# A relational graph layer on one core: edge types by transfer, a third buffer of relation rows, and one-hots in another place

## What is computed

```python
def _mgcn_conv(x, edge_index, edge_type, rel, W_in, W_out, W_loop, b, n):
    src, dst = (edge_index[0], edge_index[1])
    e = edge_index.shape[1]
    half = e // 2
    m = x[src] * rel[edge_type]
    m = jnp.concatenate([m[:half] @ W_in, m[half:] @ W_out], 0)
    deg = jax.ops.segment_sum(jnp.ones((e,), x.dtype), dst, num_segments=n)
    norm = 1.0 / jnp.maximum(deg, 1.0)
    agg = jax.ops.segment_sum(m * norm[dst][:, None], dst, num_segments=n)
    return jnp.tanh(agg + x @ W_loop + b)
...
h = emb + res * _mgcn_conv(emb, edge_index, edge_type, rel1, ...)
h = h + res * _mgcn_conv(h, edge_index, edge_type, rel2, ...)
return h @ mu_w + mu_b
```

## Time and profile before

| | us |
|---|---|
| median of three runs | 2800.0 (2799.91 to 2800.91) |
| span of the one profiled execution | 3183.3 |
| of it, edges of layer 0 and of layer 1 | 1236.8 and 1228.1 |
| of it, all other stages | 718.4 |

### The profile page before, as it was taken

The page is one execution under the profiler, slowest core; times in us unless marked ns, Lnnn a source line. Parts: engine busy times, 40 slices in busy tenths (PEclk is TensorE's granted clock), DMA queues, the critical chain, the costliest instruction groups (busy, mean ns, idle before and its releaser), DMA issues. The chain is left out here.

```text
span 3183.3 us, 55393 instructions
## 1 busy us (share of the span) xinstructions
PE 2759.1 (87%) x20688; PEld 2587.3 (81%) x20688; DVE 2303.9 (72%) x3258; ACT 1865.5 (59%) x3179; POOL 1952.0 (61%) x2129
## 2 busy tenths in 40 slices
PE   4888888888888888797888888888888887997998
PEld 3888888888888888796877887878777786997998
DVE  6777777777677777896777777777777776995665
ACT  6556665555555555585555555555555554785444
POOL 6666666666666666455666666666666664892223
PEclk9999989999999999899999999999999999998999
DMA  8333333333333333353333333333333333452221
GB/s 259 119 90 89 89 89 90 89 89 90 88 89 90 90 88 90 92 164 104 90 90 90 89 90 92 88 90 90 89 89 92 88 90 98 136 158 90 69 67 64
DMA packets 162458, 312.57 MB, mean 98 GB/s; under 512 B 34061, under 2 KB 95309, under 8 KB 162229
## 3 DMA queue, kind: packets, MB, share of 16 engines
q0 software_dynamic: 79872, 218.21, 23.8%
q1 hardware_dynamic: 81120, 89.89, 8.8%
q10 hardware_dynamic: 1237, 1.41, 0.2%
HBM read 263.90 MB, written 45.48 MB: 97 GB/s over the span
## 5 line engine op out<-in xcount | busy, mean ns | idle before, releaser
L740 PE MATMUL edge_rg<-edge_rel_hi,edge_hot 128*128 128x256 f32 x6656 | 1551.7, 293 | 86.6 <-issue 63.0
L740 PE MATMUL edge_rg<-edge_rel_lo,edge_hot 128*128 128x256 f32 x4992 | 1312.3, 289 | 60.0 <-issue 58.9
L740 PEld LDWEIGHTS edge_rg<-edge_rel_hi,edge_hot 128*128 128x128 f32 x6656 | 1219.6, 197 | 143.7 <-issue 92.2
L548 ACT ACTIVATE edge_hot<-edge_typ,minus_type 128x512 fp32r<-128x512 f32 x832 | 526.8, 685 | 935.9 <-DMA dense_prev<-emb_t 383.9
L740 PEld LDWEIGHTS edge_rg<-edge_rel_lo,edge_hot 128*128 128x128 f32 x4992 | 983.1, 197 | 70.0 <-issue 68.5
L623 DVE TENSOR_TENSOR edge_m_lo<-edge_rg,edge_m_hi 128x1024 fp32r<-128x1024 f32 x416 | 509.3, 1224 | 241.3 <-ACT edge_m_hi L541 127.7
L604 DVE TENSOR_SCALAR edge_hot<-edge_typ,type_of 128x512 fp32r<-128x512 f32 x832 | 582.3, 741 | 12.4 <-ACT edge_hot L548 8.7
L753 PE MATMUL edge_small<-edge_m_hi,edge_sel 128*128 128x258 f32 x1664 | 458.1, 306 | 96.3 <-DVE edge_m_lo L623 90.7
L530 POOL DMA_INDIRECT edge_xg<-emb,src x416 | 399.0, 959 | 225.9 <-issue 96.2
L530 POOL DMA_INDIRECT work<-h,src x416 | 400.7, 963 | 221.9 <-issue 101.9
L530 POOL DMA_INDIRECT edge_xg<-h,src x416 | 400.2, 962 | 216.2 <-issue 102.8
(11 more groups left out here) (183 smaller groups left out, 3933.9 us busy)
## 6 DMA issues: line engine op xcount, KB each, us to landing
work<-emb,src POOLq DMA_INDIRECT x416
edge_xg<-emb,src POOLq DMA_INDIRECT x416
work<-h,src POOLq DMA_INDIRECT x416
edge_xg<-h,src POOLq DMA_INDIRECT x416
set_x_rows<-in_x SPq DMA_DIRECT2D x25, 256.0 KB, 3.9
emb<-set_e_rows SPq DMA_DIRECT2D x25, 256.0 KB, 2.9
emb_t<-acc SPq DMA_DIRECT2D x5, 1280.0 KB
dense_prev<-emb_t SPq DMA_DIRECT2D x25, 256.0 KB, 2.7
```

Of the source, the lines that this page charges most:

```text
L548: act.activation(hot[:, q % 2, c], typ[q % 2][:], ACT.Abs, bias=K["minus_type"][:, c:c + 1]).then_inc(distances, 1)
L740: ins = pe.matmul(rg[q % 2][:, t, :], hot[:, q % 2, c, t * P:(t + 1) * P], part[:, c, :], start=(c == 0 and part is rel_hi), stop=(c == FULL))
```

## The change

- **Types.** The set-up stores the edge types as 16-bit integers, and SP loads those of a pair (1024 numbers) into all 128 partitions, into a tile `typ` of two buffers in SBUF, one transfer of 256 KB a pair. PE's matmul for it goes, and so do two PSUM buffers. DVE's one-hots no longer wait for ACT's distances but for that transfer, and explicitly for the relation rows that read `hot` before.
- **Three buffers of relation rows** (`RG_RING`) in place of two, in the PSUM that became free. GpSimd's gather now also waits for the message that last read its place in the ring; ACT's high part also waits for the window that last read its buffer.
- **Lags.** Message, select and low part come three turns after the one-hots (two before), the window sums five (four), the transposes and the adding six (four). PE's first window of a pair also waits for the adding of the pair before the last.
- **Order in a turn.** DVE's one-hots stand between message and select, no longer behind the low part; ACT starts its turn with the copy of the sums and the high part.

```diff
+RG_RING = 3
+SUMS_LAG = 5
+TURN_LAG = 6
...
-            act.copy(K["typ"][0:TYPE_ROWS], types_i[0:TYPE_ROWS]).then_inc(tables, 1)
+            act.copy(types_s[0:TYPE_ROWS], types_i[0:TYPE_ROWS]).then_inc(types_short, 1)
+            act.wait_ge(types_short, 1)
+            act.dma_start(types_out, types_s[0:TYPE_ROWS]).then_inc(types_stored, 16)
...
+        typ = s.sb("typ", [P, 2, 2 * GROUP * P], I16)
...
-        rg = [s.ps(f"rg{b}", [P, GROUP, DIM]) for b in range(2)]
-        typ = [s.ps(f"typ{b}", [P, GROUP * P]) for b in range(2)]
+        rg = [s.ps(f"rg{b}", [P, GROUP, DIM]) for b in range(RG_RING)]
...
+            def load_types(p):
+
+                wait_past(sp, hot_done, 2 * p - 2)
+                wait_past(sp, distances, HOT_ACT * (2 * p - 2))
+                sp.dma_start(typ[:, p % 2], types[p:p + 1, :].rearrange("o k -> (o k)").partition_broadcast(P))\
+                  .then_inc(typ_in[p % 2], 16)
...
+                wait_past(pool, messages, g - GROUPS_IN_RING + 1)
                 for t in range(GROUP):
...
+                    if bank is by_three:
+                        wait_past(act, windowed, g - 1)
...
-                act.wait_ge(typ_done, g + 1)
+                act.wait_ge(typ_in[q // 2], 16 * (i + 1))
+                wait_past(act, rel_done, g - 1)
...
-                over_groups(act, (0, later(distance)), (2, high), (0, later(one_hot)), (3, copy_sums), (0, clear_one))
+                over_groups(act, (SUMS_LAG, copy_sums), (3, high(by_three)), (0, later(distance)), (0, later(one_hot)),
+                            (0, clear_one))
...
-                dve.wait_ge(distances, HOT_ACT * (g + 1))
-
+                dve.wait_ge(typ_in[q // 2], 16 * (i + 1))
+                wait_past(dve, rel_done, g - 1)
                 for c in range(HOT_ACT, RCHUNKS):
-                    ins = dve.tensor_scalar(hot[:, q % 2, c], typ[q % 2][:], K["type_of"][:, c:c + 1], None,
+                    ins = dve.tensor_scalar(hot[:, q % 2, c], types_of(q), K["type_of"][:, c:c + 1], None,
                                             ALU.is_equal)
...
-                over_groups(dve, (2, message), (2, one_window), (4, add_window), (2, low), (0, one_hot_later))
+                over_groups(dve, (3, message(by_three)), (0, one_hot_later), (3, one_window), (TURN_LAG, add_window),
+                            (3, low(by_three)))
...
-                pe.matmul(typ[q % 2][:], row, K["typ"][0:TYPE_ROWS, q % 2 * GROUP * P:(q % 2 + 1) * GROUP * P],
-                          start=True, stop=True).then_inc(typ_done, 1)
...
+                    if q % 2 == 0:
+                        wait_past(pe, added, g // 2 - 1)
...
-                over_groups(pe, (4, one_window), (2, relation_rows), (0, spread_later), (4, turn_over))
+                over_groups(pe, (SUMS_LAG, one_window), (TURN_LAG, turn_over), (2, relation_rows(by_three)))
```

More of the change, by code:

```diff
@@ L427, in over_groups, with phase_edges @@
         turn(STEPS + t // GROUPS_IN_RING, t % GROUPS_IN_RING)
-def phase_edges(nc, K, layer, nodes, rel, nodes_t, matrices):
+def phase_edges(nc, K, layer, types, nodes, rel, nodes_t, matrices):
     first = layer == 0
@@ L465, in phase_edges @@
         rel_split = s.sem("rel_split")
-        picked = s.sem("picked")
-        typ_done = s.sem("typ_done")
+        typ_in = [s.sem(f"typ_in{b}") for b in range(2)]
         gathered = [s.sem(f"gathered{q}") for q in range(GROUPS_IN_RING)]
@@ L477, in phase_edges @@
         filled = s.sem("filled")
-        summed = s.sem("summed")
+        windowed = s.sem("windowed")
         sums_copied = s.sem("sums_copied")
@@ L505, in _ @@
                                  columns(K, chunks).rearrange("p c k n -> p c (k n)")).then_inc(columns_out, 16)
+            for p in range(2, PAIRS):
+                load_types(p)
             sp.wait_ge(messages, GROUPS - 2)
@@ L560, in copy_sums @@
                 if q % 2 == 1:
-                    act.wait_ge(summed, g // 2 + 1)
+                    act.wait_ge(windowed, g + 1)
                     act.copy(sums_sb[:, q // 2], sums[q // 2][0:WIN, :]).then_inc(sums_copied, 1)
@@ L689, in all_windows @@
                         add(0, w * WIN, half_at + w * WIN).then_inc(win_added, 1)
-                over_groups(dve, (0, pick_row), (2, message), (2, low), (0, one_hot_later), (3, all_windows),
+                over_groups(dve, (2, message(by_two)), (0, one_hot_later), (2, low(by_two)), (3, all_windows),
                             rolled=True)
@@ L726, in spread_later, with relation_rows, stage @@
-            def spread_later(g, q, i):
-                if not isinstance(g, int) or g > 1:
-                    spread_types(g, q, i)
-            def relation_rows(g, q, i):
-                if isinstance(g, int) and g == 0:
-                    pe.wait_ge(rel_split, 3)
-                    pe.wait_ge(filled, 3)
-                pe.wait_ge(hot_done, g + 1)
-                pe.wait_ge(hot_act, g + 1)
-                for t in range(GROUP):
-                    for c in range(RCHUNKS):
-                        for part in (rel_hi, rel_lo) if c < FULL else (rel_hi,):
-                            ins = pe.matmul(rg[q % 2][:, t, :], hot[:, q % 2, c, t * P:(t + 1) * P], part[:, c, :],
-                                            start=(c == 0 and part is rel_hi), stop=(c == FULL))
-                    if t < GROUP - 1:
-                        ins.then_inc(rel_tile, 1)
-                ins.then_inc(rel_done, 1)
+            def relation_rows(bank):
+                def stage(g, q, i):
+                    if isinstance(g, int) and g == 0:
+                        pe.wait_ge(rel_split, 3)
+                        pe.wait_ge(filled, 3)
+                    pe.wait_ge(hot_done, g + 1)
+                    pe.wait_ge(hot_act, g + 1)
+                    rows = rg[bank(g, q)]
+                    for t in range(GROUP):
+                        for c in range(RCHUNKS):
+                            for part in (rel_hi, rel_lo) if c < FULL else (rel_hi,):
+                                ins = pe.matmul(rows[:, t, :], hot[:, q % 2, c, t * P:(t + 1) * P], part[:, c, :],
+                                                start=(c == 0 and part is rel_hi), stop=(c == FULL))
+                        if t < GROUP - 1:
+                            ins.then_inc(rel_tile, 1)
+                    ins.then_inc(rel_done, 1)
+                return stage
@@ L1579, in build @@
 def build(nc, a, out):
+    types = nc.dram_tensor("types", [TYPE_ROWS, 2 * GROUP * P], I16, kind="Internal").ap()
     emb = nc.dram_tensor("emb", [NODES_PAD, DIM], F32, kind="Internal").ap()
```

82 lines of the change are left out of this document (42 added, 40 removed).

## The result

The changed kernel takes **2886.5 us** (2885.1 to 2887.0), the kernel before 2800.5 beside it: 1.0306 times as long, 95% interval 1.0291 to 1.0320. It is slower by 86 us. I had forecast slower at 2822, that is +22 with a range of 2670 to 2900: the sign and the range held, the size did not.

A forecast was written before the change was run, and what follows sets the result against it. GpSimd's gathers were taken to bound the kernel at 5.0 us a group, before and after. 2800 + 2 (layer starts) + 20 (one more window that delays gather starts) = 2822 us, range 2670 to 2900.

The forecast's parts named there:

- The bound: Edge stages: GpSimd's gathers set the pace, 4 x 1.25 = 5.0 us a group, with PE and DVE just below.
- 2080 + 718: Whole kernel before: 1664 gathers at 1.25 us plus the stages outside the edges, 2798 us against a median of 2800.
- Types, one-hots, third buffer, lags: PE and DVE in the edges: savings hidden under GpSimd's floor, worth 0; lag at most one turn, 5 us, a layer.
- New waits and SP's queue: Edges: waits of gathers and ACT's copy worth 0; SP's 208 transfers, 55 MB, hidden.
- 2 us for the starts of the layers: Layer starts: two type transfers ahead of the relation table, 0 to 3.9 us a layer, taken as 1, 2 us in all.
- The price of the gathers: Edges: gathers starting inside a select or SBUF one-hot are lengthened; net 20 us, bounds 0 and 146.
- net one window, 20 us: DVE in the edges: three windows instead of two, each catching 0.28 starts a group at 0.175 us, over 416 groups.
- 963 against 0.95: Gathers of before: mean 963 ns against 0.95 us, 22 us over 1664, taken to agree with 20 us for one window.
- C: Rival: GpSimd's and DVE's rhythms lock, a start falls into a one-hot's window every group; 73 to 146 us; chance 0.10.
- forecast A: The forecast itself: GpSimd bounds the kernel before and after; 2785 to 2860 us; chance 0.62.
- B: Rival: PE and DVE bound the timed runs, so the change is faster, 2592 or 2654 us; chance 0.25.
- D: Rival: one-hots also stop gathers in progress, 0.53 us a group, 221 us, 3021 us; chance 0.03.

The follow-up runs named there:

- first profile: Profile of the unchanged kernel before, taken ahead of the forecast: span 3183 us against a median of 2800.
- cut kernels: Changed kernel and kernel before, each without one of four gathers a group from the fifth group on: 2568.0 us after, 2705.0 before.
- run with the free place: Changed kernel with the select ahead of the message, waiting for the third of its group's four gathers: 2815.0 us, 1.0051.
- second profile: Kernel before, unchanged, profiled once more: span 2798.1 us.
- run with two transfers a layer: Changed kernel with type transfers for only the first two pairs of each layer (206 of 208 left out): 2885.8 us, 1.0301.
- run with DVE's old order: Changed kernel with DVE's order of before: message, select, adds, low part, one-hots: 2916.2 us, 1.0414.

## Why the prediction was right in sign and wrong in size

**The bound.** Right, and now shown and not only inferred: the 383 us of the first profile belonged to that one execution, 2080 + 718 is the time of before, and the cut kernels move with the gathers.

**Types, one-hots, third buffer, lags.** Right: worth 0 together under GpSimd's floor, within the few microseconds that the run with the free place leaves. The low part's wait of the earlier trace rows fell from 223 us (second profile) to 3.5, the one-hots take 482 ns in the median (480 forecast), and PE's and DVE's gains are there. They show only where GpSimd has room: 2705 to 2568, where I had put DVE's chain at 4.77 and PE at 4.5 a group and the runs have 4.76 and 4.4.

**New waits and SP's queue.** Right at 0: idle time between gathers is unchanged, and the run with two transfers a layer has the same time. The transfers land in 3.3 us, those of the earlier trace rows in 3.9:

```profile
edge_typ<-types SPq DMA_DIRECT2D x208, 256.0 KB, 3.3
```

I had 2 us for the starts of the layers. No run shows this term: of the 2.3 us by which the profiles differ outside the edges, 2.2 lie in the last stage.

**The price of the gathers: the step that failed.** This is the term "net one window, 20 us". The delay of one start was right (a start waits until some 0.13 us before DVE's instruction ends; 0.21 us each in after). Wrong was the number of starts: I spread them evenly and let a window catch 0.28 of them, 20 us for one window more. They are not spread. With GpSimd in the lead each start has its fixed place after the message, and a window catches one in most groups or in hardly any: 12 of 416 for before's select (2 us), 357 for after's (76 us), and 45 for the one-hots (6 us). So the term measures some 80 us in place of 20; the gathers as a whole became 81 us longer. The agreement that I leaned on, with 963 against 0.95, came from the disturbed execution, where late releases had shaken the phases: 145 starts inside selects there, 12 in the second profile. It agreed for the wrong reason.

**The rivals.** C had the mechanism (rhythms lock, because a message waits for its gather) and the price: 73 to 146 us, measured 86. It named the wrong instruction. The one-hots moved into the free place at 1.1 to 2.05 us and pushed the select out of it. I gave it 0.10, although the rule "GpSimd leads and the message waits for its landing" was in my own forecast A and makes locking the normal case. B falls with the cut kernels.

D, that gathers in progress stop too, was rightly low: the gather of 804.42 ran through a one-hot's start and took 0.94, and of the 331 in after that were 0.1 to 0.3 us under way when a pair of one-hots began none took more than 0.96. The Trainium skill, SBUF — State Buffer, section Who interferes with whom, tells of a lock that falls to whoever issues first. I had left this condition out when I took D for that rule: by it a gather in progress would hold back the one-hots. The traces show little of that: the pair at 804.60, which began during a gather, took 1.01 us in place of 0.88. The section also says that an instruction with two SBUF inputs contends with a GpSimd instruction that reads SBUF, and one in a mode that uses both ports with GpSimd at large, while one with at most one SBUF input outside those modes doesn't contend. The traces agree for the select, which held starts back with both inputs in SBUF and not with one in PSUM, and for message, low part and adds, which held back none. The SBUF one-hots held starts back and the PSUM one-hots didn't; whether the former run in such a mode, no run here shows.

**Could it have been forecast?** Nearly; one number was missing. Pitch 1.25, and a message 2.75 us behind the start of its last gather, give starts at 1.0, 2.25, 3.5 and 4.75 us. Message 1.13 and two one-hots of 0.48 put the select at 2.09, with the start at 2.25 in it. The select would end at 2.57 and let the gather begin 0.13 earlier, at 2.44: 0.19 x 416 = 79 us, a time of 2879, which is near 2886. The 2.75 was not in a row of mine, since the first profile had hardly a group in step.

## What to carry to other kernels

Where two engines are tied by a wait, their starts keep a fixed distance: don't price a collision by an even spread, but lay out one period of both and look what stands where. Moving a short instruction that costs nothing on its own engine can then cost 3% on another, and a wait that no data needs can give it back. A start that is held back costs only where others wait for that engine, so look who waits for whom before counting the delays as the price. Before relying on a profile whose span is far from the timed median, take another one.

## What the chip showed that I had not expected

The effect runs the other way too. In after an SBUF one-hot in which a gather ends takes 0.63 us on average, one without 0.48 (380 and 452 of them). In the run with DVE's old order it is only 0.50 (207 of them), so a gather's end inside is not the whole condition. Two pairs in the trace of after:

```profile
804.60 1.01 DVE L643 TENSOR_SCALAR edge_hot<-edge_typ,type_of 128x512 fp32r<-128x512 int16 x2
...
809.74 0.88 DVE L643 TENSOR_SCALAR edge_hot<-edge_typ,type_of 128x512 fp32r<-128x512 int16 x2
```

The gather of 804.42 ends at 805.36, inside the first pair; the one beside the second pair starts at 809.65 and ends at 810.73, behind it. That gather took 1.08 with a head start of 0.09 us. Ahead of a pair of one-hots a head start of 0.1 us put gathers out of reach in after, and with less 11 of 28 were lengthened. Ahead of the select of before less was enough: all 41 gathers with a head start under 0.1 us took 0.94 or 0.95 (second profile), as the one at 809.86. One-hots from PSUM take 742 ns with or without a gather's end. Why the two differ, and why it is a gather's end that lengthens a one-hot, stays open.
